# Building the first expert layer's token lists inside the experts' rounds, and a threshold search that settles two bits per round

## The reference, cut to what matters

```python
k = Sx // num_experts * CAPACITY                    # 3750 // 16 * 2 = 468
logits = jnp.einsum('bsd,de->bse', x, gate_weight)
affinity = jax.nn.softmax(logits, axis=-1).transpose(0, 2, 1)
gating, index = jax.lax.top_k(affinity, k)
x_in = jnp.take_along_axis(x[:, None, :, :], index[..., None], axis=2)
h = jax.nn.gelu(jnp.einsum('bekd,edh->bekh', x_in, w1) + b1[None, :, None, :])
x_e = jnp.einsum('bekh,ehd->bekd', h, w2) + b2[None, :, None, :]
weighted = gating[..., None] * x_e
...
out = out.at[jnp.arange(Bx)[:, None], idx_flat].add(vals_flat)
```

## Time and profile before

| | |
|---|---|
| time, median of 3 runs | 4681.58 us (4673.16 to 4683.91) |
| the profiled execution | 4665.64 us |
| its span | 4663.9 us |
| PE busy | 3144.4 us (67%) |
| DVE busy | 2371.4 us (51%) |
| POOL busy | 1556.7 us (33%) |
| w2 matmuls of the experts, L1701 | 222.5 us, x512 |
| w1 matmuls of the experts, L1693 | 206.4 us, x512 |
| gathers of the experts, L1610 | 66.4 us, x64 |

### The profile page before, as it was taken

One profiled execution on the slowest core, in us unless ns is written; L12 is line 12 of the kernel. 1 busy time (PEld: TensorE's weight loads), 2 busy tenths in 40 slices (PEclk: granted clock), 3 DMA queues, 4 the chain that ended last, 5 costly groups with the idle time before them and its releaser, 6 DMA issues. The chain is left out here.

```text
span 4663.9 us, 56101 instructions
## 1 busy us (share of the span) xinstructions
PE 3144.4 (67%) x12336; PEld 2054.9 (44%) x12337; DVE 2371.4 (51%) x4106; ACT 932.6 (20%) x2417; POOL 1556.7 (33%) x1595
## 2 busy tenths in 40 slices
PE   6193846777777785289995724974777777645991
PEld 2041424555555454164442311433555555544660
DVE  5071884555555686741113200466555555696444
ACT  2010002222222463001111200001222222341220
POOL 1616005555554100013331473003555555301225
PEclk9595977888888886569997867986888888856995
DMA  3021515555554211025555311613555555314336
GB/s 136 8 89 21 112 71 157 143 140 146 149 142 140 76 68 54 0 77 159 152 147 140 63 15 31 159 68 105 147 144 145 143 143 143 103 54 153 121 121 214
DMA packets 330645, 513.22 MB, mean 110 GB/s; under 512 B 172484, under 2 KB 177860, under 8 KB 329744
## 3 DMA queue, kind: packets, MB, share of 16 engines
q0 software_dynamic: 113824, 311.79, 25.0%
q1 hardware_dynamic: 92720, 194.54, 12.1%
q10 hardware_dynamic: 123840, 3.94, 1.5%
HBM read 423.20 MB, written 86.92 MB: 109 GB/s over the span
## 5 line engine op out<-in xcount | busy, mean ns | idle before, releaser
L890 POOL DMA_INDIRECT aggregate_zg<-z_rows,src_groups x940 | 888.3, 945 | 1395.6 <-SPq L898 594.8
L956 PE MATMUL bank<-aggregate_msg,aggregate_onehot 128*128 128x260 f32 x2816 | 824.2, 445 | 104.9 <-DVE aggregate_msg L923 80.6
L956 PEld LDWEIGHTS bank<-aggregate_msg,aggregate_onehot 128*128 128x128 f32 x2816 | 582.9, 218 | 212.3 <-issue 120.9
L923 DVE TENSOR_TENSOR aggregate_msg<-aggregate_zg,bank 128x1024 f32<-128x1024 f32 x528 | 639.1, 1210 | 8.0 <-issue 3.6
L857 ACT COPY acc<-bank x530 | 313.8, 592 | 1244.1 <-PE bank L943 694.5
L918 DVE TENSOR_SCALAR aggregate_onehot<-bank,step_base,dst_groups 128x128 f32<-128x128 f32 x704 | 256.3, 405 | 520.4 <-remote 310.2
L366 POOL DMA_INDIRECT front_d<-src_scores,src_chunks x320 | 306.2, 957 | 188.6 <-issue 97.2
L943 PE MATMUL bank<-zero_bf 128*128 128x2 bf16 x1060 | 121.0, 171 | 333.1 <-ACT acc L857 317.0
L620 PE MATMUL bank<-front_w,front_edge 128*128 128x512 f32 x360 | 197.2, 685 | 186.4 <-issue 152.9
L943 PEld LDWEIGHTS bank<-zero_bf 128*128 128x128 bf16 x1060 | 112.4, 106 | 467.4 <-issue 404.1
L1610 POOL DMA_INDIRECT exp_xg<-hn_rows,exp_gather_tok x64 | 66.4, 1038 | 659.0 <-DVE exp_gather_tok L1634 494.6
(11 more groups left out here) (373 smaller groups left out, 4306.8 us busy)
## 6 DMA issues: line engine op xcount, KB each, us to landing
exp_w<-in_L_ffn_w SPq DMA_DIRECT2D x32, 1024.0 KB
slot_out<-exp_y SPq DMA_DIRECT2D x66, 256.0 KB, 2.0
z_rows<-front_z SPq DMA_DIRECT2D x60, 256.0 KB
hn_rows<-fin_xn SPq DMA_DIRECT2D x20, 768.0 KB, 3.5
aggregate_zg<-z_rows,src_groups POOLq DMA_INDIRECT x940
front_early<-src_key SPq DMA_DIRECT2D x16, 640.0 KB
front_early<-src_tile SPq DMA_DIRECT2D x16, 640.0 KB
front_edge<-src_key SPq DMA_DIRECT2D x16, 640.0 KB
```

Of the source, the lines that this page charges most:

```text
L890: pool.indirect_dma_start(zg[:, r, j, :], None, k.z_rows[:, :], bass.IndirectOffsetOnAxis(k.src_groups[:, n:n + 1], 0)).then_inc(gathered[ ...
L923: v.tensor_tensor(msg[:, m, :, 0:HD].rearrange("p u (h d) -> p u h d", d=DH), z, bcast_last(scale[n % COEF].rearrange("p (u h) -> p u h", ...
L956: nc.tensor.matmul(k.banks[:, bank(t, half), 0:HW].rearrange("p a n -> p (a n)"), lanes_of(n % OS, j), msg[:, m, j * 2 + half, :], start=F ...
```

## The change

- The search takes 15 rounds. A round tries three thresholds at once (low bit, high bit, both bits of a pair), so that `cand`, `at_least`, `count` and `flag` have three parts; a new reduction (L1460 of the changed kernel) counts how many of the three hold, and that digit times the low bit is set. Three instructions ahead of the loop make the table of bits.
- The two blocks of lists are gone. Three lists are made at the experts' start; list e+3 is made during expert e: DVE's comparison at the start of the expert's part, PE's 30 matmuls between the second and the third quarter of w2 into bank 0, ACT's copy after its copies of transposed rows, and four small DVE instructions at the end of the expert's part (`read_list`). 12 lists are made in a loop of 6 rounds, one in a round written out, none in the last.
- The first two experts' weights, b1 and b2 are loaded from the start of the choice; both parts are one stage now (`chosen_experts`), so a barrier between stages is a block's end.

```diff
-                per = 6
-                with dve.Fori(0, 30) as b:
+                per = 7
+                with dve.Fori(0, 15) as b:
...
+                    chain(v.tensor_tensor(cand[:, :, :], thr[:, :].unsqueeze(1).to_broadcast([P, 3, E0]), bcast_last(bits, E0), ALU.bitwise_or))
+                    chain(v.tensor_tensor(at_least[:, :, :, :], aff[:, :, :].unsqueeze(1).to_broadcast([P, 3, E0, NT]),
+                                          bcast_last(cand[:, :, :].bitcast(F32), NT), ALU.is_ge))
+                    chain(v.tensor_reduce(count[:, :, :], at_least[:, :, :, :], AX, ALU.add))
...
+                    chain(v.tensor_scalar(flag[:, :, :], k.ps[0][:, 0:3 * E0].rearrange("p (d e) -> p d e", d=3), float(CAP), None, ALU.is_ge))
+                    chain(v.tensor_reduce(digit[:, :], flag[:, :, :].rearrange("p d e -> p e d"), AX, ALU.add))
+                    chain(v.tensor_tensor(bit_set[:, :], digit[:, :], low, ALU.mult))
...
+            @block.sync
+            def _(sp):
+                w1, w2, b1, b2 = k.chosen_weights
+                sp.dma_start(b1[:, :, :], I["L0_ffn_b1T"]).then_inc(k.b_loaded, 16)
+                for u in range(2):
+                    sp.dma_start(w1[:, u, :, :], I["L0_ffn_w1"].rearrange("e (c p) n -> p e c n", p=P)[u]).then_inc(k.w_loaded[u], 16)
...
+                def place_list(n, b):
+                    at = k.place[:, :, :].rearrange("p e t -> p (e t)")[:, bass.ds(n * NT, NT)]
+                    v.tensor_tensor(placed[:, b], bcast_last(at, PQ), k.iota_bf[:, 0:PQ].unsqueeze(1).to_broadcast([P, NT, PQ]),
+                                    ALU.is_equal).then_inc(placed_ready, 1)
+
+                def read_list(n, b):
+                    dve.wait_ge(list_copied, n + 1)
+                    at = bass.ds(n * Q0, Q0)
+                    v.tensor_tensor(part[:, 1, :], listed[:, b, :, 4], listed[:, b, :, 3], ALU.add)
+                    chain(v.scalar_tensor_tensor(part[:, 0, :], listed[:, b, :, 1], float(P), listed[:, b, :, 0], ALU.mult, ALU.add))
+                    v.tensor_tensor(gates[:, at], part[:, 1, :], listed[:, b, :, 2], ALU.add)
+                    chain(v.tensor_copy(tokens[:, at], part[:, 0, :]))
...
+                place_list(0, 0)
+                place_list(1, 1)
+                read_list(0, 0)
+                v.tensor_copy(gather_tok[:, 0, :], tokens[:, 0:Q0]).then_inc(gather_tok_ready, 1)
+                dve.wait_ge(list_summed, 1)
+                place_list(2, 0)
+                read_list(1, 1)
+                v.tensor_copy(gather_tok[:, 1, :], tokens[:, Q0:2 * Q0]).then_inc(gather_tok_ready, 1)
+                read_list(2, 2)
...
+                        if u < lists:
+                            take_list(i * U + (u + AHEAD0), 0, AHEAD0 + u)
...
+                def sum_list(n, bank, b):
+                    pe.wait_ge(placed_ready, n + 1)
+                    for t in range(NT):
+                        mm = nc.tensor.matmul(k.ps[bank][0:PQ, 0:Q0 * 5], placed[:, b, t, :],
+                                              k.by_quarter[:, bass.ds(n, 1), t, :, :].rearrange("p a q f -> p (a q f)"),
+                                              start=(t == 0), stop=(t == NT - 1))
+                    mm.then_inc(list_summed, 1)
...
+                            if q == 1 and u < lists:
+                                pe.wait_ge(xg_t_ready, i * (U * Q0) + (u * Q0 + Q0 + 1))
+                                sum_list(i * U + (u + AHEAD0), 0, (u + AHEAD0) % 2)
```

More of the change, by code:

```diff
@@ L1435, in _ @@
                 chain(v.tensor_tensor(by_expert, by_expert, bcast_last(vm1[:, :], E0), ALU.add))
-                per = 6
-                with dve.Fori(0, 30) as b:
-                    chain.enter(b, per)
[L1441 to L1444, removed]
+                pairs = k.bits[:, :].rearrange("p (r b) -> p r b", b=2)
@@ L1626, in _ @@
                     gather(u, u)
-                rounds(pool, body)
+                with pool.Fori(0, ER - 1) as i:
+                    body(i, False)
+                body(ER - 1, True)
             @block.vector
@@ L1662, in take, with take_list, body @@
                                        k.ps[q][:, 0:KC * PQ].rearrange("p (c n) -> p c n", c=KC)).then_inc(xg_t_ready, 1)
-                def body(i, last):
+                def take_list(n, bank, b):
+                    act.wait_ge(list_summed, n + 1)
+                    nc.scalar.copy(listed[:, b, :, :].rearrange("p q f -> p (q f)"), k.ps[bank][0:PQ, 0:Q0 * 5]).then_inc(list_copied, 1)
+                def body(i, lists, last):
                     for u in range(U):
@@ L1670, in body @@
                             take(i * U + (u + 1))
-                act.wait_ge(b_loaded, 16)
+                        if u < lists:
+                            take_list(i * U + (u + AHEAD0), 0, AHEAD0 + u)
+                for n in range(AHEAD0):
+                    take_list(n, n, n)
+                act.wait_ge(k.b_loaded, 16)
                 take(0)
-                rounds(act, body)
+                with act.Fori(0, LISTING) as i:
+                    body(i, U, False)
+                body(LISTING, 1, False)
+                body(ER - 1, 0, True)
             @block.tensor
@@ L1680, in turn @@
                     for q in range(Q0):
-                        if h_count is not None:
+                        if h_count is None:
+                            pe.wait_ge(list_copied, min(q + 1, AHEAD0))
+                        else:
                             pe.wait_ge(h_done, h_count + (q + 1))
@@ L1690, in body @@
                         pe.wait_ge(xg_t_ready, i * (U * Q0) + (u * Q0 + Q0))
+                        if not last:
+                            pe.wait_ge(list_copied, i * U + (u + AHEAD0))
                         for f in range(F):
```

163 lines of the change are left out of this document (71 added, 92 removed).

## The result

The changed kernel takes 4608.99 us (median of 4 runs, 4605.86 to 4623.34), the kernel before in the same session 4677.37 (4 runs, 4662.21 to 4683.91): ratio 0.9864, 95% interval 0.9831 to 0.9897. The medians differ by 68.4 us; the ratio, which goes by the means, makes it 63.6 (the prediction said 61.2). Of the 11 us between 4620 and 4609, 4 come from the kernel before, which took 4677.37 here where the forecast started from 4681.58. The profiled execution took 4610.76 us, 54.9 less than before's 4665.64.

A forecast was written before the change was run, and what follows sets the result against it. The choice was taken as bound by a chain of short steps, the experts' rounds by PE. Search -13.8, start -71.0 and lists +23.6 sum to -61.2 us, giving 4620 us; own range 4608 to 4634, 8 times in 10 4602 to 4655.

The forecast's parts named there:

- The bound of the rounds: Experts' rounds: PE is the only bound, busy 350.6 of 351.3 us, so all array time added there is paid.
- The search: Search loop of the choice: 15 rounds of 5.67 us instead of 30 of 3.31, saving 13.8 us.
- The rival in which it gains nothing: Search: three-fold broadcasts run at 1.5 ns an element, 13.8 us saved turns into -6, total 4640 us; chance 4%.
- The start: Experts' start: first comparison to first transposes takes 17.4 us instead of 88.4, saving 71.0 us.
- the gather, 7.9 us from its issue: Experts' start: with weights loaded earlier, the first gather takes 7.9 us from issue instead of 12.8.
- The lists in the rounds: Middle of w2 on PE: 12 looped lists at 1.9 us and one written out at 0.8 cost 23.6 us.
- 0.025 us a pair: Array time for a list's load and matmul, taken from 128x30 pairs; 30 make 0.8 us for the written-out list.
- the sequencer's share, 1.9: Looped list: 16 or 17 of 30 pairs queued, the rest at 0.13 us each, 1.9 us a list.
- Rival one: Lists in the rounds: the queue hides the whole list, costing 10 us instead of 23.6, total 4607 us; chance 12%.
- Rival two: Lists in the rounds: semaphore waits stop the sequencer running ahead, costing 49 us instead of 23.6, total 4646; chance 17%.
- The rival of a fall after each list: Rounds: PE's clock falls after lists, 1.7 us lost each fall, total 4632 or 4668 us; chance together 10%.
- the slower one built on it: Rounds: clock falls with a long warm-up, 13 lists at 8.9 us cost 116, total 4713 us; chance 4%.

The follow-up runs named there:

- search-only run: The kernel before with the new two-bit search alone, lists and experts as before: 4662.37 us, ratio 0.9968 to the kernel before.
- the run with the steps in PSUM: The changed kernel with the third list's comparison reading its row of numbers 0 to 116 from PSUM instead of SBUF: 3638.28 us on the third chip.
- late-weights run: The changed kernel with the first two experts' weights loaded at the experts' start again instead of at the choice's start: 4607.02 us.
- both edits: The changed kernel with the list's weight columns padded from 117 to 128 and its moving operand copied to a fixed place: 4634.47 us, ratio 0.9855 to before.
- the other execution of the changed kernel: The changed kernel run again without any edit, on the third chip: 3643.68 us, ratio 0.9841 to the kernel before.

## Why the prediction was right, point by point

- **The bound of the rounds** held: PE is busy all of 355.50 us, and whatever array time a list takes is paid in full. The 49 us more of DVE work cost nothing.
- **The search** came out to a tenth: 1.04 ns an element carries over from 480 and 2048 elements to a threefold broadcast of 1440 (1658 ns, and 1653 for the reduction). The rival in which it gains nothing fell with that row, and by the search-only run.
- **The start** was 2.4 us short of the forecast. The step that failed is "the gather, 7.9 us from its issue": I took the time of a gather that ran alone, and here POOL's instruction for it lay beside a DVE comparison and took 3.68 us. That cause is shown, by the run with the steps in PSUM. I also named the early weights as what makes the gather short; the late-weights run shows that in the changed kernel they aren't needed for it.
- **The lists in the rounds**: 22.5 for 23.6, and the agreement is partly luck. That before's pace of 0.13 us was not the array's is right: at the same clock of 0.50, without addresses, the changed kernel's first list took 3.17 us for 30, 0.106 apiece. The step that failed is the next one, which gave the array 0.025 us a pair: that came from 128 columns, and a list has 117. It made 0.8 us of the written-out list, which took 1.68. For the looped ones two errors met: I had the array too fast, and the sequencer's share, 1.9, a little too dear. Some 18 pairs are given out ahead, as the earlier trace rows let one work out; only the list doesn't wait for the rest as long as the columns are 117. Rival one (the queue hides the whole list, 28.7 us a period) named the right figure for a kernel that has both edits. (The Trainium skill's page "TensorE: Matmul & The Clock Gate", the specifications ahead of Part 1, has a queue of 64; 18 pairs are 36 entries, and from 2028.9 on, 6 us before the list, the sequencer gave out one address per pass of 0.43 us, as if it had no room for more; so this trace stays against all 30 pairs being in it.) Rival two fell: the sequencer did run ahead behind its waits, its first address at 2028.4 for a list that began at 2035.35.
- **The clock** was 1.00 in all rounds. The rival of a fall after each list, and the slower one built on it, did not occur at 1.65 us; at 3.8 us a fall does occur, and costs 1.7 us.
- **What I left out** is the clock at the start of the experts: it was worth 2.6 us here, and 1.0 in the other execution of the changed kernel. Why it rose sooner after the transposes here isn't shown. Term by term I missed by +2.4, -1.1, -2.6 and -0.1 us; they cancel to -1.4, and that is luck too.

## What to carry to other kernels

Work moved into a stage that one engine bounds is paid there in full however small its instructions are, so price it by the same shape: the pace of 128 weight columns said nothing of 117. Where a stage doesn't respond to the removal of its suspected bound, look for a second one of the same size before calling the first harmless; here each of two edits gave nothing and both gave 0.9 us a list. And when a transfer starts late, see what the neighbouring engine was doing while it was being issued.

## What the runs showed of the hardware

- A bfloat16 weight load with its matmul of 20 columns takes 0.0545 us for 117 weight columns and 0.025 for 128, at a clock of 1.00. At 0.50 the first list of the changed kernel, of 117, took 3.17 us for 30.
- An address that depends on the loop's counter costs PE's sequencer 0.124 us a matmul, and the sequencer was 18 of the list's matmuls ahead of the array when the array came to the list.
- DVE's comparison with two inputs in SBUF holds POOL's indirect-DMA instructions: 3.68 us for 0.99, and 4.00 for the changed kernel's fifth beside the fourth comparison (1976.90 to 1980.72), for both 2-byte and 4-byte inputs; with one input in PSUM it doesn't.

```profile
1977.57 4.00 POOL L1575 DMA_INDIRECT exp_xg<-hn_rows,exp_gather_tok  x1 [0.30 <-issue]
```

- The same program took 4677 and 4705 us on two chips and 3703 on a third (the kernel before; the changed one 4609 on the first and 3644 on the third). The stretch studied is the same in both (624.61 and 625.71 us). Of the 967 us between the two profiled executions some 560 lie in the two stages that aggregate rows by indirect gathers (875 and 879 us against 596 and 598, with 142 GB/s moved against 209) and some 400 in the stages ahead of them (481 and 677 us against 275 and 481). The gather's line on the profile's page in the long run and in the short one: instructions of the same length, 1389.7 and 550.7 us of idle time ahead of them.

```profile
L890 POOL DMA_INDIRECT aggregate_zg<-z_rows,src_groups x940 | 890.9, 948 | 1389.7 <-SPq L898 583.3
```
```profile
L890 POOL DMA_INDIRECT aggregate_zg<-z_rows,src_groups x940 | 888.8, 946 | 550.7 <-issue 283.6
```

Why the program is quicker on that chip stays open; no run tested it.
